# Score maxima of two heads in one reduction over both PSUM banks; first loads, a small product and the written orders changed with it

## The chip, the cores and the metric

One core of a Trainium2 chip runs the kernel. The metric is the device time of one execution in microseconds (us); lower is better. A profile of one execution stands beside the times.

## What is computed

The input is 64 sequences of 64 channels and 256 positions. They go through four sub-layers in a row: an 8-head cross-attention with rotary positions, a feed-forward layer with ternary weights and 8-bit activations, a one-head cross-attention with a mask, and a gated feed-forward layer with ternary weights by groups of 64.

```python
# sub-layer A, heads of 8 channels: the part that the change touches
scores = einsum('bhtc,bhsc->bhts', q, k) / sqrt(8)
p      = softmax(scores, axis=-1)          # the kernel takes a row maximum out before exp
out    = einsum('bhts,bhsc->bhtc', p, v)
# sub-layer B: the scales of the 8-bit activations that the small product feeds
gamma_x = clip(max(abs(x), -1), 1e-5);  gate = silu(bit_linear(x, gate_w));  val = bit_linear(x, val_w)
y = bit_linear(gate * val, out_w)          # its scale contains gamma_x squared
```

## The kernel before, in words

Two sequences make a pair, whose 128 channels fill the partitions; there are 32 pairs. Every engine works through a list of named steps such as `mx3:7` (step kind `mx`, part 3, pair 7). The lists are written out by hand for each engine: HEAD for the first pairs, ORDER for a steady period that LOOP repeats with a growing pair number, and TAIL for the last pairs. The order on an engine is fixed by its list; semaphores between the kinds of steps hold a step until what it needs is there. The SP list issues nearly all DMAs.

For a pair the chain is: load and normalise (`xP`, `bsP`, `mvP`, `rsP`, `xnP`), projections (`proj`, `v`), rotary (`r1`, `r2`, `rot`, `hi`, `lo`, and `kq`, six DMAs into KQ), scores for the maxima (`S`, 16 heads of the pair, line 617), their row maxima (`mx`, line 1120), the maxima turned and put back into KQ as one more row (`mxp`, `mxc` line 804, `md`), scores again the other way round with the maximum subtracted (`T`, line 625), exp (`E`, line 799), probabilities times values (`pv`, line 639), the division (`u`, `sg`, `rc`, `or`, `om`), output projection (`y`, `x1`). Sub-layer B follows three periods behind (`bsB`, `sxB`, `xr`, `xq`, `bg`, `bv`, `Bg`, `Bv` line 691, `Bd`), then the second attention (`xcT`, `sc`, `wx`, `pD`, `pT`, `ro`), then sub-layer C (`Cg`, `Cu` line 728, `Cd` line 739) up to seven periods behind, and `st` stores the pair.

PSUM has eight banks of 512 fp32 columns. Two hold the first scores (`psS`), two the second (`psT`), four all else (`psW`; BANKS says which step uses which of the four). `S` of head n writes 128 x 512 scores of one head (two matmuls of 256 columns) into bank n % 2 of psS, and `mx` of head n reduces that bank to two maxima per partition:

```python
after(pe, "mx", p, n - 2)                                  # line 614: S of head n waits for mx of head n - 2
after(dve, "S", p, n)                                      # line 1117: mx of head n waits for S of head n
m = nc.vector.tensor_reduce(mx[:, p % 2, :, 4 * (n % 4) + n // 4],
                            psS[:, n % 2, :].rearrange("p (c s) -> p c s", c=NK), AX.X, ALU.max)
```

So one bank is filled while the other is reduced. `sxB` (lines 1186 to 1197) makes the scales of sub-layer B in instructions on one column; the second product of them is a SCALAR_TENSOR_TENSOR with two tensors in SBUF (line 1195).

At the start SP loads the table with the identity (`tab`), the biases, the small weights (`wsm`), the first x and the first context; ACT issues at once the six weight loads of 1 MB each (lines 746 to 755). TensorE, VectorE and GpSimd each wait for all set-up work before their first listed step. Ternary weights are made from the raw ones between the steps of the first pairs (`c`, `ab`, `ra`, `gm`, `gv`, `qa`, `rn`, `cl`, `qb`, `fx`, `tn`, `tc`, `fr`, `ct`).

## Time and profile before

| | |
|---|---|
| median of 3 runs | 837.59 us (830.35 to 840.47) |
| the profiled execution | 840.63 us, its span 838.8 us |
| busy share of the span, PE / DVE / ACT / POOL | 91% / 90% / 84% / 76% |
| `psS` maxima, line 1120 | 512 instructions, 333.3 us busy |
| SCALAR_TENSOR_TENSOR of line 1195 | 32 instructions, 20.8 us busy |

The span runs from the first to the last instruction. A busy share counts an instruction from its start to its end, also where the next one has begun, so that a busy engine can still hold work that would fit closer. TensorE's matmuls overlap, and two score matmuls in different row groups run side by side.

### The profile page before, as it was taken

The page shows a single profiled execution, that of the slowest core. Times are in us where ns is not written, and L with a number is a line of the kernel's source. Part 1 is how long each engine was busy: PE and PEld are TensorE (multiplying, and loading weights), DVE is VectorE, ACT ScalarE, POOL GpSimd, SP SyncE. Part 2 cuts the span into 40 slices and gives each one's busy share as a digit, 9 for nine tenths or more (in the row PEclk, how much of TensorE's full clock was granted, in tenths as well). Part 3 has the DMA queues.
Part 4 walks back from the last instruction along what each step waited for, and adds up shares of the span by engine and source line. Part 5 has one row for each costly group of instructions (what it writes and reads, how often), then busy time and mean ns, then how long its engine had stood idle before and what let it go on. Part 6 is the DMA issues. An engine that isn't in the chain of part 4 may idle for free. (4 is left out here: it accounts for less than half of the span.)

```text
span 838.8 us, 22126 instructions
## 1 busy us (share of the span) xinstructions
PE 763.0 (91%) x6898; PEld 398.9 (48%) x6898; DVE 752.7 (90%) x1636; ACT 701.4 (84%) x1447; POOL 634.2 (76%) x1139
## 2 busy tenths in 40 slices
PE   2677899999999999999999999999999989898886
PEld 1333444454555554555555555555545445444444
DVE  5688899999899999999999999999989989787865
ACT  3888888888799998999989999999979889688644
POOL 3827566788888887888888888888878877677632
PEclk9557899999999999999999999999999999899989
DMA  9401222244443444454544444544443434344230
GB/s 311 133 21 39 59 75 77 65 114 88 94 115 95 115 97 106 109 112 108 113 109 106 112 110 114 115 99 112 109 97 101 104 84 112 72 91 97 57 69 20
DMA packets 197952, 82.59 MB, mean 98 GB/s; under 512 B 139710, under 2 KB 196670, under 8 KB 197836
## 3 DMA queue, kind: packets, MB, share of 16 engines
q1 hardware_dynamic: 193260, 74.63, 38.1%
q10 hardware_dynamic: 4576, 6.55, 2.4%
q8 instruction: 56, 0.92, 0.5%
q14 instruction: 60, 0.49, 0.2%
HBM read 28.15 MB, written 4.69 MB: 39 GB/s over the span
## 5 line engine op out<-in xcount | busy, mean ns | idle before, releaser
L1120 DVE TENSOR_REDUCE mx<-psS 128x2 f32<-128x512 f32 x512 | 333.3, 679 | 21.0 <-PE psS L617 19.9
L799 ACT ACTIVATE prob<-psT 128x512 f32<-128x512 f32 x512 | 292.4, 603 | 23.2 <-PE psT L625 15.4
L617 PE MATMUL psS<-KQ 31*128 31x256 f16 x1024 | 137.7, 284 | 15.1 <-DVE mx L1120 12.1
L639 PE MATMUL psW<-prob,vst 128*32 128x256 f32 x2048 | 143.0, 400 | 0.0
L728 PE MATMUL psW<-guT,xT 128*128 128x512 bf16 x512 | 133.5, 390 | 6.3 <-DMA xT<-stage 5.1
L625 PE MATMUL psT<-KQ 32*128 32x256 f16 x1024 | 129.4, 280 | 3.9 <-ACT prob L799 3.0
L639 PEld LDWEIGHTS psW<-prob,vst 128*32 128x32 f32 x2048 | 55.2, 112 | 61.5 <-issue 34.6
L728 PEld LDWEIGHTS psW<-guT,xT 128*128 128x128 f16 x512 | 43.3, 99 | 72.8 <-issue 38.8
L1004 POOL TENSOR_TENSOR hqB<-wide,rnd 128x512 bf16<-128x512 f32 x60 | 63.4, 1058 | 14.7 <-ACT wide L847 14.4
L617 PEld LDWEIGHTS psS<-KQ 31*128 31x128 f16 x1024 | 40.0, 93 | 72.4 <-DVE mx L1120 46.1
L1018 POOL TENSOR_TENSOR stage<-stage 128x512 f16<-128x512 f32 x60 | 69.6, 1161 | 2.6 <-ACT stage L908 0.5
L691 PE MATMUL psW<-tern,xqT 128*128 128x512 bf16 x256 | 70.5, 389 | 0.0
L739 PE MATMUL psW<-pT,stage 128*128 128x256 bf16 x512 | 66.0, 273 | 2.0 <-DMA stage<-stage 1.4
L625 PEld LDWEIGHTS psT<-KQ 32*128 32x128 f16 x1024 | 42.1, 93 | 44.6 <-ACT prob L799 27.0
L739 PEld LDWEIGHTS psW<-pT,stage 128*128 128x128 f16 x512 | 47.8, 98 | 18.2 <-issue 6.6
L1243 DVE SCALAR_TENSOR_TENSOR stage<-stage,psW 128x512 f32<-128x512 f32 x64 | 43.1, 681 | 14.2 <-ACT stage L900 13.4
L813 ACT COPY uA<-psW 128x512 f32<-128x512 f32 x64 | 37.7, 588 | 19.9 <-PE psW L639 19.8
L652 PE MATMUL psW<-cP,wsm 128*128 128x256 f32 x128 | 46.9, 451 | 7.4 <-DMA cP<-in_ctx 6.4
L842 ACT ACTIVATE stage<-psW,sB 128x512 f32<-128x512 f32 x64 | 44.0, 688 | 11.3 <-PE psW L691 9.8
L900 ACT ACTIVATE stage<-psW 128x512 f32<-128x512 f32 x64 | 38.0, 595 | 17.8 <-PE psW L728 17.6
L998 POOL TENSOR_TENSOR r<-pc,tab 128x512 f32<-128x512 f32 x32 | 40.7, 1273 | 15.3 <-ACT pc L818 15.3
L847 ACT ACTIVATE wide<-wide,sB 128x512 f32<-128x512 f32 x64 | 46.6, 733 | 0.4 <-DVE sB L1220 0.2
(190 smaller groups left out, 1791.0 us busy)
## 6 DMA issues: line engine op xcount, KB each, us to landing
KQ<-hl SPq DMA_DIRECT2D x192, 64.0 KB, 1.9
xP<-in_x SPq DMA_DIRECT2D x32, 128.0 KB, 2.2
cP<-in_ctx SPq DMA_DIRECT2D x32, 128.0 KB, 2.1
xA<-in_x SPq DMA_DIRECT2D x32, 128.0 KB, 2.6
cB<-in_ctx SPq DMA_DIRECT2D x32, 128.0 KB, 2.3
oV<-uA SPq DMA_DIRECT2D x32, 128.0 KB, 2.1
out<-x SPq DMA_DIRECT2D x32, 128.0 KB, 2.1
oR<-rden_d SPq DMA_DIRECT2D x120, 32.0 KB
```

Of the source, the lines that this page charges most:

```text
L617: m = nc.tensor.matmul(psS[:, n % 2, T * k:T * k + T], KQ[p % DEEP][r, 1, g, 128 * k:128 * k + 128], KQ[p % DEEP][r, 0, g, :], start=True, ...
L625: m = nc.tensor.matmul(psT[:, n % 2, T * k:T * k + T], KQ[p % DEEP][r, 0, g, 128 * k:128 * k + 128], KQ[p % DEEP][r, 1, g, :], start=True, ...
L639: m = nc.tensor.matmul(bank[32 * j:32 * j + 32, :], vst[p % DEEP][:, k, 4 * n + j, :], prob[:, (4 * n + j) % 8, k, :], start=(k == 0), sto ...
L652: m = nc.tensor.matmul(bank[:, T * f:T * f + T], wqk[:, j, :], (cP, xnP)[f][:], start=True, stop=True)
L691: m = nc.tensor.matmul(psW[:, BANK[f"{kind.lower()}{n}"], :], xqT[:, k, :], (gT if kind == "Bg" else vT)[:, k, 512 * n:512 * n + 512], sta ...
L728: m = nc.tensor.matmul(bank, xT[:, NK * part + k, :], w[:, k, :], start=(k == 0 and part == 0), stop=(k == NK - 1 and part == 1))
L739: m = nc.tensor.matmul(psW[:, BANK["Cd0"], 0:T], hT[:, 8 * part + c, :], pT[:, c, :], start=(c == 0 and part == 0), stop=(c == 7 and part ...
L799: m = nc.scalar.activation(flat(prob[:, n % 8, :, :]), psT[:, n % 2, :], ACT.Exp, scale=float(HC) ** -0.5)
L847: m = nc.scalar.activation(hrB[:, 512 * n:512 * n + 512], hB[:, 512 * n:512 * n + 512], ACT.Copy, scale=sB[:, p % 2, 8:9], bias=ROUND)
L1004: m = nc.gpsimd.tensor_tensor(hqB[:, h], hrB[:, h], rnd[:].broadcast_to([P, 512]), ALU.subtract)
L1018: m = nc.gpsimd.tensor_tensor(hhl[:, 1, n, :], hC[:, n, :], hhl[:, 0, n, :], ALU.subtract)
L1120: m = nc.vector.tensor_reduce(mx[:, p % 2, :, 4 * (n % 4) + n // 4], psS[:, n % 2, :].rearrange("p (c s) -> p c s", c=NK), AX.X, ALU.max)
```

## The change

Two heads are reduced by one instruction of 128 x 1024 over both banks of psS, which writes four maxima per partition; there are 8 of them in a pair and not 16. `S` of heads 2n and 2n+1 wait for the maxima of the two heads before them, and a reduction waits for both of its heads. psS still has two banks. The product of line 1195 becomes a TENSOR_SCALAR, whose two factors are both pointer scalars (one tensor, two columns). At the start, x comes first and the table last on SP; ACT waits for the biases and small weights, then issues two weight loads, and the other four become steps `wl` in its list; TensorE does its first projections and `v` before it waits for the table; the identity copies of GpSimd (`id`) and two of the three memsets of vst (`vm`) become steps. All five lists and the table of banks are written anew. The new kind `hot` stands in no list.

```diff
-PARTS = {**{k: NH for k in ("S", "mx", "T", "E")}, "pv": NG,
+PARTS = {**{k: NH for k in ("S", "T", "E")}, "mx": NH // 2, "pv": NG,
...
-SET_POOL, SET_DVE = 13, 2 * DEEP + 2
+SET_POOL, SET_DVE = 13, DEEP + 3
 ORDER = {
-    "pe": """ro:-5 pv0:-1 T6:-1 S8:0 T7:-1 bg0:-3 S9:0 proj0:2 Bg0:-3 S10:0 T8:-1 T9:-1 S11:0 pv1:-1 Bd:-4 bv0:-3
-           S12:0 bv1:-3 S13:0 T10:-1 bg1:-3 T11:-1 Bv0:-3 Bg1:-3 Bv1:-3 S14:0 T12:-1 S15:0 T13:-1 y:-2 proj1:2 mxp:0
-           T14:-1 S0:1 S1:1 T15:-1 pv2:-1 Cg0:-5 pv3:-1 tn0:0 tn4:-4 Cg1:-5 xcT:-4 gm:1 S2:1 T0:0 S3:1 T1:0 Cu0:-5
-           v:2 sc:-4 S4:1 T2:0 S5:1 T3:0 tn2:-2 Cu1:-5 tn1:-1 tn3:-3 tn5:-4 Cd0:-6 pT:-4 S6:1 T4:0 S7:1 T5:0 Cd1:-6""",
-    "dve": """mx6:0 x4:-7 bsP:3 x3:-5 mx7:0 bsC:-5 fx2:-4 mx8:0 mx9:0 ct0:-2 ct1:-2 mvC:-5 cl1:0 r1:2 mx10:0 mx11:0
-           aB0:-3 mvP:3 x2:-4 mx12:0 mx13:0 bsD:-4 hB0:-3 mvD:-4 cl0:1 ra2:1 mx14:0 ct2:-2 mx15:0 aB1:-3 bsB:-2
-           cl2:-1 hB1:-3 fx1:-1 mvB:-2 fx0:0 mx0:1 val:2 amH:-3 mx1:1 ra1:2 sx:-3 gv:1 aC0:-5 amB:-2 aC1:-5 mx2:1
-           mx3:1 sxB:-2 wx:-4 mx4:1 mx5:1 bs:0 rc:-1 hC0:-5 hC1:-5 ra0:3""",
...
+    "pe": """pv2:-2 Cg0:-6 pv3:-2 Cg1:-6 S2:0 S3:0 T0:-1 gm:0 T1:-1 xcT:-5 v:1 Cu0:-6 sc:-5 S4:0 S5:0 T2:-1 tn3:-4
+           T3:-1 tn0:-1 Cu1:-6 tn4:-5 tn5:-5 Cd0:-7 tn2:-3 T4:-1 S6:0 S7:0 T5:-1 pT:-5 Cd1:-7 ro:-5 pv0:-1 T6:-1
+           T7:-1 S8:0 S9:0 bv0:-3 bg0:-3 proj0:2 Bg0:-3 T8:-1 T9:-1 tn1:-2 S10:0 S11:0 pv1:-1 Bd:-4 T10:-1 S12:0
+           S13:0 bv1:-3 T11:-1 bg1:-3 Bv0:-3 Bg1:-3 Bv1:-3 T12:-1 S14:0 S15:0 T13:-1 y:-2 proj1:2 mxp:0 T14:-1 S0:1
+           T15:-1 S1:1""",
+    "dve": """mvB:-3 ct0:-1 amH:-4 cl1:-1 mx0:0 fx0:-1 ct2:-3 sx:-4 aC0:-6 amB:-3 mx1:0 sxB:-3 hC0:-6 wx:-5 mx2:0
+           aC1:-6 ra2:1 fx2:-4 rc:-2 ra0:2 gv:0 cl0:1 hC1:-6 mx3:0 x4:-7 bsP:3 cl2:-2 x3:-5 bsC:-5 mx4:0 mvC:-5 r1:2
+           mx5:0 aB0:-3 mvP:3 ct1:-2 ra1:2 x2:-4 mx6:0 bsD:-4 hB0:-3 mvD:-4 bs:-2 mx7:0 fx1:-1 aB1:-3 bsB:-2 hB1:-3
+           val:2""",
...
-    "dve": """bsP:0 mvP:0 r1:0 ra0:0 bsP:1 mvP:1 bsP:2 mvP:2 ra1:0 r1:1 mx0:0 mx1:0 mx2:0 gv:0 mx3:0 mx4:0 mx5:0 mx6:0
-           mx7:0 cl0:0 mx8:0 bs:0 mx9:0 mx10:0 mx11:0 mx12:0 bsP:3 mx13:0 r1:2 mx14:0 mvP:3 mx15:0 fx0:0 mx0:1 mx1:1
...
+    "dve": """bsP:0 mvP:0 vm0:0 r1:0 ra0:0 bsP:1 mvP:1 ra1:0 bsP:2 r1:1 mvP:2 ra2:0 mx0:0 mx1:0 mx2:0 mx3:0 gv:0 mx4:0
+           bsP:3 mvP:3 r1:2 mx5:0 cl0:0 mx6:0 mx7:0 vm1:0 mx0:1 fx0:0 bsP:4 mx1:1 mx2:1 r1:3 mx3:1 mx4:1 mvP:4 cl1:0
+           mx5:1 bs:0 mx6:1 mx7:1 val:0 mx0:2 mx1:2 ct0:0 mx2:2 cl2:0 mx3:2 rc:0 mx4:2 ct1:0 fx1:0 r1:4 mx5:2 mx6:2
+           ct2:0 bsP:5 mvP:5 bsB:0 mvB:0 mx7:2 amB:0 mx0:3 sxB:0 mx1:3 mx2:3 rc:1 mx3:3 mx4:3 bsP:6 mx5:3 mx6:3 r1:5
...
+    "act": """xnP:0 wl0:0 vst:0 wl1:0 c0:0 pc:0 wl2:0 c1:0 hi:0 xnP:1 wl3:0 c2:0 ab0:0 pc:1 ab1:0 vst:1 ab2:0 xnP:2
+           rn0:0 hi:1 rn1:0 xnP:3 fr0:0 pc:2 mxc:0 md:0 rn2:0 E0:0 E1:0 E2:0 E3:0 vst:2 E4:0 E5:0 E6:0 fr1:0 E7:0
...
-BANKS = ("v tn0 tn1 bv1 tn5 Cg1 Cd0 lh0 lh1 lx",
-         "proj0 gm mxp y Bd tn4 Cg0 Cu1 lz0",
-         "pv2 bg0 bg1 tn3 ro Cu0",
-         "proj1 pv0 tn2 bv0 xcT sc pT lq lz1")
+BANKS = ("v pv0 bv1 tn4 Cg0 Cu1 lq lh1 lz0",
+         "proj0 mxp y tn2 Bd ro Cg1 lx",
+         "gm tn0 pv2 tn1 bg0 bg1 tn3 tn5 Cu0 Cd0",
+         "proj1 bv0 xcT sc pT lh0 lz1")
...
-            sp.dma_start(tab[:], c_tab).then_inc(S["tab_in"], 16)
+            sp.dma_start(xP[:], x_p[0]).then_inc(S["xP"], 16)
             sp.dma_start(small[:], biases).then_inc(S["c_in"], 16)
             sp.dma_start(wsm[:], w_small).then_inc(S["c_in"], 16)
-            sp.dma_start(xP[:], x_p[0]).then_inc(S["xP"], 16)
             sp.dma_start(cP[:], ctx_p[0]).then_inc(S["cP"], 16)
+            sp.dma_start(tab[:], c_tab).then_inc(S["tab_in"], 16)
...
-            pe.wait_ge(S["tab_in"], 16)
-            pe.wait_ge(S["set_pool"], SET_POOL)
             pe.wait_ge(S["set_dve"], SET_DVE)
-
+            settled = False
+
+            hot_banks = iter(HOT_BEFORE)
             for name, kind, n, p in PROGRAM["pe"]:
+                if not settled and kind not in ("proj", "v"):
+                    pe.wait_ge(S["tab_in"], 16)
+                    pe.wait_ge(S["set_pool"], SET_POOL)
+                    settled = True
...
-                    after(pe, "mx", p, n - 2)
+                    after(pe, "mx", p, n // 2 - 1)
...
-                    after(pe, "mx", p, NH - 1)
+                    after(pe, "mx", p, NH // 2 - 1)
...
+            act.wait_ge(S["c_in"], 16 * 2)
             for i, (raw, part) in enumerate(((stage[:, 3, :], gu_w[0:HID, :]), (late[0], gu_w[HID:2 * HID, :]))):
                 nc.scalar.dma_start(raw.rearrange("p (r d) -> p r d", r=8), part.rearrange("(r p) d -> p r d", p=P))\
                     .then_inc(S[f"w1_{i}"], 16)
-            nc.scalar.dma_start(late[1].rearrange("p (r h) -> p r h", r=2), p_w.rearrange("(r p) h -> p r h", p=P))\
-                .then_inc(S["w1_2"], 16)
-            for i, w in enumerate((gate_wT, val_wT)):
-                nc.scalar.dma_start(stage[:, i, :].rearrange("p (k h) -> p k h", k=2),
-                                    w.rearrange("(k p) h -> p k h", p=P)).then_inc(S[f"w0_{i}"], 16)
-            nc.scalar.dma_start(stage[:, 2, :].rearrange("p (k d) -> p k d", k=8),
-                                out_wT.rearrange("(k p) d -> p k d", p=P)).then_inc(S["w0_2"], 16)
-            act.wait_ge(S["c_in"], 16 * 2)
...
+                if kind == "wl":
+                    raw, w = ((late[1].rearrange("p (r h) -> p r h", r=2), p_w.rearrange("(r p) h -> p r h", p=P)),
+                              (stage[:, 0, :].rearrange("p (k h) -> p k h", k=2), gate_wT.rearrange("(k p) h -> p k h", p=P)),
+                              (stage[:, 1, :].rearrange("p (k h) -> p k h", k=2), val_wT.rearrange("(k p) h -> p k h", p=P)),
+                              (stage[:, 2, :].rearrange("p (k d) -> p k d", k=8),
+                               out_wT.rearrange("(k p) d -> p k d", p=P)))[n]
+                    nc.scalar.dma_start(raw, w).then_inc(S[("w1_2", "w0_0", "w0_1", "w0_2")[n]], 16)
...
+                    if 0 < p < DEEP:
+                        act.wait_ge(S["set_dve"], SET_DVE + p)
...
-            for i in range(DEEP):
-                nc.vector.memset(vst[i][:], 1.0).then_inc(S["set_dve"], 1)
+            nc.vector.memset(vst[0][:], 1.0).then_inc(S["set_dve"], 1)
             nc.vector.memset(ones[:], 1.0 / (T * HID)).then_inc(S["set_dve"], 1)
             nc.vector.memset(brow[:], 0.0).then_inc(S["set_dve"], 1)
             dve.wait_ge(S["c_in"], 16 * 2)
-            dve.wait_ge(S["tab_in"], 16)
             dve.wait_ge(S["bv_ready"], 1)
             nc.vector.tensor_tensor(bo_c[:], psW[:, 0, 0:1], small[:, 4:5], ALU.add).then_inc(S["set_dve"], 1)
             dve.wait_ge(S["set_dve"], SET_DVE)
-            dve.wait_ge(S["set_pool"], SET_POOL)
 
...
+                if kind == "vm":
+                    nc.vector.memset(vst[n + 1][:], 1.0).then_inc(S["set_dve"], 1)
+                    continue
...
-                    after(dve, "S", p, n)
+                    after(dve, "S", p, 2 * n + 1)
                     if n == 0:
                         after(dve, "mxp", p - 2)
-                    m = nc.vector.tensor_reduce(mx[:, p % 2, :, 4 * (n % 4) + n // 4],
-                                                psS[:, n % 2, :].rearrange("p (c s) -> p c s", c=NK),
-                                                AX.X, ALU.max)
+                    first = 8 * (n % 2) + n // 2
+                    m = nc.vector.tensor_reduce(mx[:, p % 2, :, first:first + 5:4].rearrange("p c h -> p h c"),
+                                                psS[:].rearrange("p h (c s) -> p h c s", c=NK), AX.X, ALU.max)
...
-                    nc.vector.scalar_tensor_tensor(out=sc[:, 5:6], in0=sc[:, 1:2], scalar=sc[:, 1:2],
-                                                   in1=gam_q[:, 1:2], op0=ALU.mult, op1=ALU.mult)
+                    nc.vector.tensor_scalar(sc[:, 5:6], sc[:, 1:2], sc[:, 1:2], gam_q[:, 1:2], ALU.mult, ALU.mult)
```

## Rows read from the trace of the kernel before

**Rows 1.** The page's first part: busy time, share of the span, instructions.
```profile
PE 763.0 (91%) x6898; PEld 398.9 (48%) x6898; DVE 752.7 (90%) x1636; ACT 701.4 (84%) x1447; POOL 634.2 (76%) x1139
```

**Rows 2.** Stages by `mxs`: count, duration min/median/max, first and last start.
```profile
L804 ACT ACTIVATE mxs<-psW x10: 356/372/373, 49.7 to 246.2; 16x256 f16<-16x256 f32 x10
...
L804 ACT ACTIVATE mxs<-psW x17: 372/372/373, 246.2 to 602.3; 16x256 f16<-16x256 f32 x17
...
L804 ACT ACTIVATE mxs<-psW x7: 356/372/373, 602.3 to 745.2; 16x256 f16<-16x256 f32 x7
```

**Rows 3.** Stretches: length, busy of PE, PEld, DVE, ACT, POOL; clock, DMA, GB/s.
```profile
50.00:246.00 196.00, 181.80 (x1638) 88.71 (x1636) 177.41 (x367) 167.43 (x331) 137.87 (x225) 0.91 0.31 74
246.00:602.00 356.00, 347.02 (x3394) 187.51 (x3392) 348.59 (x785) 325.35 (x705) 308.53 (x561) 1.00 0.47 108
602.00:745.00 143.00, 135.26 (x1259) 68.68 (x1257) 128.95 (x286) 119.67 (x261) 110.19 (x203) 0.96 0.42 97
745.00:839.00 94.00, 75.98 (x546) 42.61 (x544) 64.73 (x137) 57.75 (x127) 50.02 (x107) 0.95 0.29 65
```

**Rows 4.** The same view, four steady periods: the first, and the sum.
```profile
492.10:514.10 22.00, 21.68 (x216) 11.76 (x220) 21.63 (x50) 20.33 (x45) 19.28 (x35) 1.00 0.46 112
...
sum 87.90, PE 86.86 PEld 47.00 DVE 86.59 ACT 81.42 POOL 77.11; mean PE 21.71 PEld 11.75 DVE 21.65 ACT 20.36 POOL 19.28
```

**Rows 5.** Waits from 470 to 580 us: in total, times, longest.
```profile
POOL rsC L958 <- DVE mvC L1171: 3.2, 5, 0.9
...
PE psW L716 <- ACT pD L887: 1.0, 3, 0.4
...
PEld psS L617 <- DVE mx L1120: 5.4, 14, 0.4
```

**Rows 6.** Groups by form: busy, mean ns, idle before and its releaser.
```profile
L1120 DVE TENSOR_REDUCE mx<-psS 128x2 f32<-128x512 f32 x512 | 333.3, 679 | 21.0 <-PE psS L617 19.9
...
L1185 DVE TENSOR_REDUCE sB<-wide 128x1 f32<-128x1024 f32 x32 | 38.7, 1208 | 0.1
...
L1195 DVE SCALAR_TENSOR_TENSOR sB<-sB,gam_q 128x1 f32<-128x1 f32 x32 | 20.8, 649 | 0.0
```

**Rows 7.** Timeline: start, length, engine, line, operation.
```profile
404.34 1.21 DVE L1185 TENSOR_REDUCE sB<-wide 128x1 f32<-128x1024 f32 x1
...
405.47 0.68 DVE L1120 TENSOR_REDUCE mx<-psS 128x2 f32<-128x512 f32 x1
...
408.47 1.28 DVE L1120 TENSOR_REDUCE mx<-psS 128x2 f32<-128x512 f32 x2
...
409.49 1.27 POOL L1010 TENSOR_TENSOR rot<-r 128x512 f32<-128x512 f32 x1
...
409.67 0.14 DVE L1193 TENSOR_SCALAR sB<-sB 128x1 f32<-128x1 f32 x1
...
409.98 0.80 DVE L1195 SCALAR_TENSOR_TENSOR sB<-sB,gam_q 128x1 f32<-128x1 f32 x1
...
410.70 0.15 DVE L1197 RECIPROCAL sB<-sB 128x1 f32<-128x1 f32 x1
```

**Rows 8.** Lines 1195 and 1194, each: duration ns min/median/max, first and last start.
```profile
L1195 DVE SCALAR_TENSOR_TENSOR sB<-sB,gam_q x32: 208/765/1057, 97.9 to 782.1; 128x1 f32<-128x1 f32 x32
...
L1194 DVE TENSOR_SCALAR sB<-sB,gam_q x32: 212/214/216, 97.7 to 782.0; 128x1 f32<-128x1 f32 x32
```

**Rows 9.** Timeline of the start, with the idle time before in brackets.
```profile
9.35 0.59 PE L587 MATMUL psW<-small,wsm 128*128 128x1 f32 x2 [9.35 <-DMA wsm<-in_w_small]
...
10.08 0.16 DVE L1057 TENSOR_TENSOR bo_c<-psW,small 128x1 f32<-128x1 f32 x1 [3.46 <-PE psW L587]
...
23.15 1.19 PE L652 MATMUL psW<-cP,wsm 128*128 128x256 f32 x2 [6.41 <-DMA cP<-in_ctx]
...
28.32 0.39 PE L617 MATMUL psS<-KQ 31*128 31x256 f16 x4 [1.41 <-DMA KQ<-hl]
...
32.71 0.59 PE L602 MATMUL psW<-wsum,ones 128*128 128x4 f32 x2
```

## What the change was predicted to do

> **What bounds the kernel now.** I read the page's busy shares first. TensorE (PE) and VectorE (DVE) are both at 90% or a little more, ScalarE (ACT) is at 84% [rows 1], so the shares alone do not name a bound. Next I cut the span by stage, with the maxima product `mxs` as the clock of the pairs [rows 2]. The first comes at 49.7 us. Nine more pairs take 196.5 us (21.8 each), the repeated order's sixteen pairs take 356.1 us (22.3 each), the last six take 142.9 us (23.8 each), and 93.6 us of the span follow the last maxima. In the repeated part PE and DVE are both busy 98%, in the two parts around it DVE is at 90 to 91% and PE at 93 to 95% [rows 3]. In four undisturbed periods of 22.0 us, DVE has 0.3 us idle and PE 0.26 us [rows 4].
>
> So I looked at how much of these busy times must be there. DVE's do not add up without gaps: two maxima back to back start at 408.47 and the next instruction starts at 409.67, so one occupies DVE for 0.60 us, though it is listed with 0.68 [rows 7]. In PE the waits of weight loads tell more than its busy time: in five periods they wait 5.4 us for maxima, and PE itself 1.0 us for `pD` [rows 5]. DVE paces the loop, with PE close behind it. GpSimd (POOL) waits little for anyone, and it works through chains of small dependent steps. Its 19.3 us of 22.0 leave at most 2.7 us, and ACT's 20.4 us leave 1.6 [rows 4].
>
> **The maxima.** 512 instructions of 512 columns become 256 of 1024. The trace has a reduction of 1024 columns, in SBUF: listed 1208 ns [rows 6], and the next instruction starts 1.13 us after it [rows 7]. Two maxima occupy 1.20 us, so each pair of heads saves 0.07 us, which makes 0.56 us in a pair and 18 us in all. By listed durations it would be 2 x 679 - 1208 = 150 ns, 38 us in all. The lower end is nothing, if crossing the bank or writing four scattered maxima costs as much as one start. I take 18, because occupancy is what an engine at 98% gives back.
>
> Here a rule of the Trainium skill can be weighed ("VectorE: DVE Perf Modes", the section on the TRN2 errata): it gives a VectorE instruction from PSUM 120 cycles plus its columns, at 0.96 GHz. Its 120 cycles would save 0.125 us in a pair of heads, an estimate of 32 us in all. The rows show that half of this already overlaps with the neighbour.
>
> **The small product.** Line 1195 takes 649 ns in the mean, 765 in the median and 208 at least [rows 6, 8]. In the timeline it starts at 409.98 while POOL's 128x512 sum runs from 409.49 to 410.76, and it ends at 410.78 [rows 7]: it waits for POOL. The TENSOR_SCALAR before it, on the same columns, takes 212 to 216 ns in all 32 pairs, whatever POOL does [rows 8]. The new form is the same kind with a second pointer scalar. I price it at 0.21 us: 20.8 - 32 x 0.21 = 14 us. The ends are 0, if it waits for POOL too, and 18 us by the median. The page "SBUF — State Buffer" of the Trainium skill (section on the two separate sides) says that VectorE and GpSimd share one pair of ports by an exclusive lock, taken by a VectorE instruction with two SBUF tensors or in a 2-port perf mode. For line 1195 the trace agrees; should the new TENSOR_SCALAR run in such a mode, the rule would take the 14 us away, and line 1194 is the row against that.
>
> DVE thus loses 0.56 + 0.44 = 1.0 us in a pair, and needs about 21 us where it had 22.
>
> **The bank that no longer alternates.** A pair of heads now needs: both maxima done, four matmuls of `S`, the reduction. Four such matmuls take 0.39 us [rows 9], and a handover from PE to DVE 0.14 us (9.94 to 10.08) [rows 9], so a refill that nothing covers costs DVE 0.39 + 2 x 0.14 = 0.67 us. Before, the other bank's reduction covered it. The new DVE list puts other work between the maxima: `hC0 wx`, `aC1 rc hC1`, `x4 bsP x3 bsC`, `mvC r1`, `aB0 mvP x2` and so on. The shortest of these gaps, `mvC r1`, holds 2 x 0.4 us and a small one, so each is longer than a refill. On PE the new list has about 2 us of other work between two blocks of `S`, which is longer than the 1.2 us of a reduction with its two handovers. In the loop I charge nothing. If that cover went in one of eight, it would be 0.67 us in a pair, 21 us in all. In pair 0 there is no cover: `mx0` to `mx3` stand together in the list. I charge 8 x 0.4 = 3 us there, between 0 and 8 x 0.67 = 5.
>
> **What PE can take.** The gain of the loop ends where PE ends. The certain part is its idle 0.26 us [rows 4]. The upper end adds the weight loads' wait for maxima, 5.4 / 5 = 1.1 us [rows 5], most of which lies under running matmuls. The new PE list also moves `pT` a block of scores further from `sc`, so that its wait for `pD` (1.0 / 5 = 0.2 us) should go, and keeps more scores in blocks. I take 0.6 us in a period, between 0.26 and 1.0 (all that DVE gives). Sixteen pairs: 10 us. Nine pairs before them, where DVE also makes the ternary weights: 0.55 each, 5 us. The last six, with DVE at 90%: 0.5 each, 3 us. After the last maxima no term of the change is left but the new lists; DVE has 29 of 94 us idle there [rows 3]. I charge 0, within 4 us either way.
>
> **The start.** The first matmul waits until 9.35 us for the small weights, which share the queues with 6 MB of raw weights, and the second context holds PE for 6.4 us until 23.15 [rows 9]. With the raw weights behind the small ones the first should come some 4 us earlier. The product over all weight sums (32.71 us, line 602) waits for the last raw weight [rows 9], and the same bytes must arrive, now issued later; pair 0 has it in the middle of its scores. So a part of the 4 us comes through, and I take 6 us for the queue and the second context together, less the 3 us above: 3 us net, between -3 and +7. The four weight loads are now steps in ACT's list and cost it their issue; the moved memsets and copies are the same instructions later, under the loads. SP's and POOL's lists have the same steps in another order and can hold one another; that, and the new table of banks, is in the range.
>
> **Sum.** 10 + 5 + 3 + 3 = 21 us less than the profiled execution's 840.6, 819.6. The median of the runs lies 3.0 below that execution: 817.
>
> **Rivals.**
> - All that DVE gives arrives (PE's list packs better): 1.0 us x 31 pairs = 31, and 6 at the start: 37 less, 801 on the median. For it: the weight loads' waits. Against it: ACT with 20.4 of 22.0, which would be at 97%. Chance 0.17.
> - PE is the bound already: only 0.26 us x 31 = 8, and 2 at the start: 827. For it: PE's 98.8% in four periods. The same time results if the joined reduction saves nothing or the new product waits for POOL, so the case that the change doesn't do what it says is in here. Chance 0.28.
> - The single set of banks decides: PE and DVE take turns. Its place is the refill inside a pair; its price 0.67 us for each uncovered one against 1.0 us saved per pair, so it decides from two in eight on. With half of them uncovered, 4 x 0.67 - 1.0 = 1.7 us in a pair in the loop and less than half of that elsewhere, some 35 us in all with nothing at the start: 872; with three, 20: 857. DVE's 19.9 us of waiting for scores, with two banks, speak for it [rows 6]. The Trainium skill ("Trainium Kernel Development and Optimization", Best Practices) advises double buffering, which is this rival's side. Chance 0.10, and I give it 860.
> - My forecast: 0.45, its own range 808 to 828.
>
> **Numbers.** A difference under 2% (16.8 us, 820.8 to 854.3) can't be told from no change in this kernel. Faster by more: 0.65 of my case, all of the first rival, little of the second: 0.49. Slower: two thirds of the third: 0.08. Within: 0.43. The range leaves out half of the best case below and the turn-taking above: 800 to 841.
>
> **What would show it.** Line 1120 with 256 instructions of about 1.21 us, the next instruction starting 1.13 us on; its replacement of line 1195 at 0.21 us in every pair; `mxs` 21.6 us apart in the loop; PE's idle under 0.2 us in a period, DVE's idle near 1 us, put down to scores (line 617) or projections. A first matmul near 5 us. Wrong would be a period of 22 us or more with DVE waiting for scores before most reductions, a reduction above 1.36 us, the product still at 0.6 us, or a clock below 1.00 in the loop.

## The result and the profile after

| | before | after |
|---|---|---|
| median | 837.36 us (830.35 to 840.47, 4 runs) | 845.18 us (841.00 to 847.11, 4 runs) |
| ratio, 95% interval | | 1.0128 [1.0079, 1.0176] |
| the profiled execution's span | 838.8 us | 842.1 us |

The changed kernel is slower by one per cent, a difference that these runs separate from zero though it is under 2%: its fastest execution is slower than the slowest of the kernel before. The forecast was 817 us and the range ended at 841. Medians are of all runs, while the ratio is an estimate from the fast ones and not the quotient of the two medians (1.0093 here). The two profiled executions lie 3.3 us apart by their spans where the medians lie 7.8 apart, so the stages below account for part of the loss.

The page's busy times of the kernel after (engine, us, share, instructions), beside [rows 1]:

```profile
PE 749.6 (89%) x6898; PEld 394.2 (47%) x6898; DVE 728.5 (87%) x1380; ACT 698.7 (83%) x1447; POOL 633.5 (75%) x1139
```

Its groups by form (busy, mean ns, idle before and the releaser), beside [rows 6]:

```profile
L1140 DVE TENSOR_REDUCE mx<-psS 128x4 f32<-128x1024 f32 x256 | 311.5, 1217 | 38.4 <-PE psS L628 37.7
...
L1216 DVE TENSOR_SCALAR sB<-sB,gam_q 128x1 f32<-128x1 f32 x32 | 8.5, 265 | 0.0
```

The work did fall as intended: VectorE is busy 24.2 us less. The time did not follow. What VectorE lost in work it spends waiting, 17.8 us of it for scores (37.7 us after 19.9). The stages by `mxs`, beside [rows 2] (count, duration, first and last start):

```profile
L816 ACT ACTIVATE mxs<-psW x10: 357/373/374, 47.6 to 248.7; 16x256 f16<-16x256 f32 x10
...
L816 ACT ACTIVATE mxs<-psW x17: 373/373/374, 248.7 to 611.6; 16x256 f16<-16x256 f32 x17
...
L816 ACT ACTIVATE mxs<-psW x7: 357/373/373, 611.6 to 751.5; 16x256 f16<-16x256 f32 x7
```

The first comes 2.1 us earlier, nine pairs take 201.1 us instead of 196.5, the sixteen of the loop 362.9 instead of 356.1, the last six 139.9 instead of 142.9, and 90.6 us of the span follow instead of 93.6. So the loop lost 6.8 us where it was to give 10. Its stretch in the view of stretches, beside [rows 3]:

```profile
248.00:611.00 363.00, 341.89 (x3394) 185.07 (x3393) 336.12 (x658) 324.44 (x706) 308.26 (x561) 1.00 0.49 106
```

TensorE did the same 3394 matmuls at the full clock (1.00, 2.4 GHz) and has fallen from 97 to 94% busy, VectorE from 98 to 93%. Nobody is at a bound; everybody waits for somebody. These are the waits of the loop (248 to 611 us) with a named releaser, in the kernel after: in total, times, longest.

```profile
POOL xqB L1000 <- DVE sB L1217: 23.5, 16, 3.5
...
PE psW L739 <- DMA xT<-stage: 15.4, 16, 2.5
ACT stage L914 <- PE psW L739: 13.5, 14, 2.7
DVE mx L1140 <- PE psS L628: 11.4, 16, 2.0
DVE stage L1263 <- ACT stage L914: 11.0, 11, 2.6
```

The same view of the kernel before, over its loop (248 to 602 us):

```profile
DVE stage L1243 <- ACT stage L900: 3.4, 6, 1.0
...
PE psW L728 <- DMA xT<-stage: 1.2, 2, 0.7
```

Read them as a chain. The gate matmuls of layer C wait once in every pair for the transpose `xT` (15.4 us, before 1.2). ScalarE waits for those matmuls and VectorE for ScalarE, VectorE's list is late, and GpSimd waits for its `sxB` once in every pair. SP in turn waits once in every pair for what GpSimd and ScalarE make of it, `xqB` (248 to 610 us):

```profile
SPq L337 <- POOL xqB L1004: 16.6, 16, 1.1
...
SPq L561 <- ACT xqB L850: 13.4, 16, 0.9
```

The scores' share, 11.4 us in 16 pairs of 8 reductions, is small: a turn-taking over the banks would show here, and in TensorE's waits for `mx`, of which this stretch has none; neither shows. The transpose is issued by SP. Its timeline in one period of the kernel after (start, length, queue, line, operation):

```profile
415.47 1.25 SPq L561 DMA_TRANSPOSE xqT<-xqB  x1
416.82 0.53 SPq L543 DMA_DIRECT2D rden_d<-rden  x1
417.44 0.59 SPq L531 DMA_DIRECT2D oV<-uA  x1
418.12 1.27 SPq L565 DMA_TRANSPOSE hqT<-hqB  x1
419.48 2.85 SPq L548 DMA_DIRECT2D oR<-rden_d  x4
422.44 3.82 SPq L527 DMA_DIRECT2D KQ<-hl  x6
426.30 0.59 SPq L579 DMA_DIRECT2D out<-x  x1
427.06 2.25 SPq L571 DMA_TRANSPOSE xT<-stage  x1
```

And TensorE at its end:

```profile
431.06 1.02 PE L739 MATMUL psW<-guT,xT 128*128 128x512 bf16 x4 [0.27 <-DMA xT<-stage]
```

From the transpose of `xqB` on, SP issues 16 transfers one behind the other with at most 0.17 us between two, and `xT` is the last of them, 11.6 us after the first. The one ahead of it is the store of pair p-8, for which nobody stands waiting here: 0.59 us and a small gap, 0.76 us in all. In the old list the store stood near the beginning:

```diff
-    "sp": """xP:4 cP:3 st:-8 sm:9 ov:-1 d1:-1 qT:-2 ht:-3 or:-1 kq:2 xT:-4 cB:-3 xA:0 hT:-5 br:-1 sg:0""",
+    "sp": """xP:3 qT:-3 d1:-2 ov:-2 ht:-4 or:-2 kq:1 st:-8 xT:-5 xA:-1 br:-2 sm:26 cB:-4 hT:-6 sg:-1 cP:3""",
```

Together with the waits above this reads as a circuit: `xT`, gate matmuls, ScalarE, VectorE, `sxB`, GpSimd, `xqB`, SP's issues, `xT`. In a circuit every 0.76 us is paid in every pair. That is theory L, after the lists: the place of the transpose in SP's list costs the time. Theory B, after the banks, was the prediction's third rival: the single set of banks costs.

### The profile page after: what moved, and what is told of

The parts are those of the page before. It is cut to its first block and busy times, and to the rows that moved or that the text cites. A ratio compares the mean times of both kernels' runs of the same rounds, so it can differ in the third digit from the quotient of the medians.

```text
span 842.1 us, 21875 instructions
## 1 busy us (share of the span) xinstructions
PE 749.6 (89%) x6898; PEld 394.2 (47%) x6898; DVE 728.5 (87%) x1380; ACT 698.7 (83%) x1447; POOL 633.5 (75%) x1139
## 5 line engine op out<-in xcount | busy, mean ns | idle before, releaser
L1140 DVE TENSOR_REDUCE mx<-psS 128x4 f32<-128x1024 f32 x256 | 311.5, 1217 | 38.4 <-PE psS L628 37.7
L739 PE MATMUL psW<-guT,xT 128*128 128x512 bf16 x512 | 135.6, 395 | 23.4 <-DMA xT<-stage 22.9
L628 PE MATMUL psS<-KQ 31*128 31x256 f16 x1024 | 111.9, 282 | 22.3 <-DVE mx L1140 12.3
L636 PEld LDWEIGHTS psT<-KQ 32*128 32x128 f16 x1024 | 39.6, 93 | 70.4 <-ACT prob L811 43.4
L1023 POOL TENSOR_TENSOR hqB<-wide,rnd 128x512 bf16<-128x512 f32 x60 | 63.4, 1060 | 11.6 <-ACT wide L861 11.6
L628 PEld LDWEIGHTS psS<-KQ 31*128 31x128 f16 x1024 | 33.8, 93 | 61.3 <-DVE mx L1140 29.6
L750 PEld LDWEIGHTS psW<-pT,stage 128*128 128x128 f16 x512 | 50.0, 100 | 13.1 <-DVE stage L1271 2.0
L1033 POOL TENSOR_TENSOR hl<-rot,hl 128x512 f16<-128x512 f32 x32 | 37.1, 1159 | 24.7 <-ACT hl L842 21.8
L1271 DVE SCALAR_TENSOR_TENSOR stage<-stage,hsc,psW 128x512 f32<-128x512 f32 x64 | 45.9, 718 | 5.4 <-PE psW L739 3.7
```

Source lines behind the costliest of these rows:

```text
L628: m = nc.tensor.matmul(psS[:, n % 2, T * k:T * k + T], KQ[p % DEEP][r, 1, g, 128 * k:128 * k + 128], KQ[p % DEEP][r, 0, g, :], start=True, ...
L636: m = nc.tensor.matmul(psT[:, n % 2, T * k:T * k + T], KQ[p % DEEP][r, 0, g, 128 * k:128 * k + 128], KQ[p % DEEP][r, 1, g, :], start=True, ...
L739: m = nc.tensor.matmul(bank, xT[:, NK * part + k, :], w[:, k, :], start=(k == 0 and part == 0), stop=(k == NK - 1 and part == 1))
L750: m = nc.tensor.matmul(psW[:, BANK["Cd0"], 0:T], hT[:, 8 * part + c, :], pT[:, c, :], start=(c == 0 and part == 0), stop=(c == 7 and part ...
L1023: m = nc.gpsimd.tensor_tensor(hqB[:, h], hrB[:, h], rnd[:].broadcast_to([P, 512]), ALU.subtract)
L1140: m = nc.vector.tensor_reduce(mx[:, p % 2, :, first:first + 5:4].rearrange("p c h -> p h c"), psS[:].rearrange("p h (c s) -> p h c s", c=N ...
```

## The experiments

All of them, each with its median, its ratio to the kernel before run beside it on the same chip (whose median was 833.86 to 835.42 us beside e1 to e15), the loop's sixteen pairs by `mxs`, and TensorE's wait for `xT` in the whole execution (us, times). The last two columns are of the one profiled execution, which lies up to 5.8 us from the kernel's median (e11 5.8 and e5 5.5 us above, e3 3.3 and e1 3.2 us below):

| kernel | median | ratio, 95% interval | loop | `xT` |
|---|---|---|---|---|
| before | 837.36 | | 356.1 | 5.1, 6 |
| after | 845.18 | 1.0128 [1.0079, 1.0176] | 362.9 | 22.9, 23 |
| e1 before, new product | 829.79 | 0.9923 [0.9886, 0.9959] | 347.1 | 3.4, 3 |
| e2 before, joined | 905.96 | 1.0855 [1.0800, 1.0910] | 363.4 | 2.0, 2 |
| e3 after, split | 839.74 | 1.0061 [1.0024, 1.0098] | 359.6 | 19.0, 20 |
| e4 after, `xT` before `st` | 824.35 | 0.9871 [0.9830, 0.9911] | 349.1 | 9.8, 11 |
| e5 e4, split | 825.37 | 0.9858 [0.9810, 0.9906] | 353.8 | 8.1, 7 |
| e6 e4, old product | 824.84 | 0.9870 [0.9814, 0.9926] | 345.4 | 9.1, 9 |
| e7 `xT` before `kq` | 913.14 | 1.0910 [1.0857, 1.0963] | 429.8 | 5.9, 5 |
| e8 before, `st` late | 1037.68 | 1.2408 [1.2344, 1.2473] | 559.3 | 5.6, 3 |
| e9 `st` last | 825.59 | 0.9905 [0.9874, 0.9937] | 347.4 | 7.0, 7 |
| e10 `xA` before `xT` | 846.15 | 1.0134 [1.0096, 1.0172] | 365.8 | 26.5, 22 |
| e11 before, `cB` before `xT` | 847.92 | 1.0174 [1.0134, 1.0214] | 370.7 | 16.9, 15 |
| e12 e4, head changed | 826.49 | 0.9906 [0.9872, 0.9940] | 350.1 | 7.6, 8 |
| e13 e4, split, old product | 824.66 | 0.9888 [0.9854, 0.9922] | 348.7 | 7.1, 8 |
| e14 after, `d1 ov` first | 858.87 | 1.0309 [1.0267, 1.0350] | 379.2 | 19.7, 19 |
| e15 e4, `d1 ov` first | 846.35 | 1.0159 [1.0124, 1.0194] | 372.7 | 5.3, 5 |

**What stands ahead of the transpose.** e4 exchanges two entries of SP's repeated list:

```diff
-or:-2 kq:1 st:-8 xT:-5 xA:-1
+or:-2 kq:1 xT:-5 st:-8 xA:-1
```

> The changed kernel with two entries of SP's steady list exchanged, so that the transpose of xT (pair p-5) is issued before the store of pair p-8 instead of behind it. Theory L: xT is issued about 0.6 us earlier in each of 16 loop pairs, gate/up matmuls wait less for it (22.9 us falls towards 13), and the time falls by 3 to 8 us, to 837 to 842. Theory B: the wait for xT was in the shadow of the scores, and the time stays within 2 us of 845.

It gave far more than expected: 0.9871 against the changed kernel's 1.0128, some 21 us. In its loop the transpose now follows `kq` at once, and the waits of the circuit went together:

```profile
POOL xqB L1000 <- DVE sB L1217: 7.7, 11, 1.8
...
DVE mx L1140 <- PE psS L628: 5.0, 12, 0.7
PE psW L739 <- DMA xT<-stage: 4.8, 5, 2.0
...
ACT stage L914 <- PE psW L739: 3.3, 4, 1.5
...
DVE stage L1263 <- ACT stage L914: 1.9, 3, 1.1
```

The wait for scores fell with them, though the banks are the same single set, so it was mostly a consequence. The loop gained 13.8 us, 0.86 in each pair, near the 0.76 that was moved. The remaining 6 us lie outside the loop, where the lists are the same: 1.1 less in the nine pairs, 2.3 in the last six, 1.2 behind them and 1.6 at the start. The stages there vary by 2 or 3 us among kernels with the same lists, so I assign them to nothing. TensorE's granted clock does not explain the 21 us: three of e4's six executions have a mean of 0.952 to 0.956, as the four of the kernel after (0.949 to 0.955), and take 822 to 826 us against 841 to 847. e10 puts another transfer there and takes the store away, e9 takes the store to the end of the list:

```diff
-or:-2 kq:1 st:-8 xT:-5 xA:-1 br:-2
+or:-2 kq:1 xA:-1 xT:-5 st:-8 br:-2
```

> The changed kernel with the store out of the way but another load, xA of 0.57 us on SP, in its place ahead of the transpose of xT. Theory L (any issue of 0.6 us there costs the same, whatever it moves): about 845 us again, 838 to 848, with about 20 waits for xT of about 20 us in sum. Rival (it was the store itself, through the buffer x4 or the DMA traffic that it makes at that time): 822 to 829 us, as in e4.

```diff
-kq:1 st:-8 xT:-5 xA:-1 br:-2 sm:26 cB:-4 hT:-6 sg:-1 cP:3
+kq:1 xT:-5 xA:-1 br:-2 sm:26 cB:-4 hT:-6 sg:-1 cP:3 st:-8
```

> The changed kernel with the store of pair p-8 at the very end of SP's steady list, behind cP, where SP waits for others anyway, so that neither xT nor hT stands behind it. Theory L (only the place of the transpose in SP's chain mattered, and PE bounds the loop once it is early): the same as with the store right behind xT, 820 to 827 us. Rival (SP's chain still bounds the loop at 21.5 us a period): the 0.6 us per period that the store takes goes as well, 810 to 819 us.

Side by side on one chip they came out at 846.15 and 825.59 us, with 18.4 us between their loops, 1.15 a pair. It is not the store, its bytes or its buffer: another issue of 0.6 us in that place costs the same 20 us. And behind the transpose the store's place makes no difference that can be measured (e4 and e9). e11 tries the same in the old lists, with the old reductions:

```diff
-or:-1 kq:2 xT:-4 cB:-3 xA:0 hT:-5
+or:-1 kq:2 cB:-3 xT:-4 xA:0 hT:-5
```

> The kernel before with the load cB (0.58 us on SP) and the transpose of xT exchanged in SP's steady list. In the trace of before the gate matmuls start 3.0 us after the transpose's issue, which lands about 0.5 us ahead of them, so a shift of 0.6 us just uses up the slack. Theory L: 835 to 845 us with 10 to 20 waits for xT of 5 to 15 us, a smaller loss than in the new lists because the old ones leave 0.5 us. Rival (the old lists bear it, VectorE bounds their loop): within 0.4% of before.

It lost 14.6 us in its loop, 0.9 a pair, and took over the sign of the kernel after (in the whole execution; 11 of the waits are in the loop):

```profile
PE psW L728 <- DMA xT<-stage: 16.9, 15, 2.2
```

So the loss needs neither the join nor the new lists; the slack of 0.5 us that I had granted the old ones did not soften it.

The circuit can be measured in SP's timelines of the loop (means of its 16 pairs, worked out from the starts and the landings). From the issue of the transpose of `xqB` to the landing of `xT` it takes 15.4 us in the kernel after and 15.5 in e10, 14.1 in e4 and in e9; from that landing round to the next transpose of `xqB` it takes 7.5, 7.4, 7.6 and 7.5 us. In the old lists the two parts are 13.0 and 9.3 us before, 14.0 and 9.4 in e11. The rest of the round stays as it is, and the whole part in which the transfer was put ahead is added to the period. This also answers why the price is above 0.76 us: of the 1.24 us between the kernel after and e4, 0.65 is the later issue, and 0.59 is that the transpose lands later after its issue. In the view of `xT` over the loop, the kernel after and then e4:

```profile
DMA to landing us min/median/max: 2.5/2.8/4.7
```

```profile
DMA to landing us min/median/max: 2.5/2.5/4.0
```

Right behind the store, `xA` or `cB` (the kernel after, e3, e10, e11, e14) the mean is 2.9 to 3.3 us, and 4 to 8 of 16 transposes take over 3 us; right behind the copies to KQ (the kernel before, e1, e2, e4 to e6, e9, e12, e13, e15) it is 2.5 to 2.7 us, with 1 to 3 of 16. Where SP pauses ahead of it, 11 us in e8 and 3 us in e7, the mean is 2.5. What holds the transpose up behind another transfer was not tested.

**What the join and the product are worth.** e1 and e2 put each alone into the kernel before, e3 takes the join out of the one after:

```diff
-nc.vector.scalar_tensor_tensor(out=sc[:, 5:6], in0=sc[:, 1:2], scalar=sc[:, 1:2],
-                               in1=gam_q[:, 1:2], op0=ALU.mult, op1=ALU.mult)
+nc.vector.tensor_scalar(sc[:, 5:6], sc[:, 1:2], sc[:, 1:2], gam_q[:, 1:2], ALU.mult, ALU.mult)
```

> The kernel before with one edit: the product of line 1195 as a tensor_scalar with two pointer scalars. Both theories expect the same of it, since it is common ground: the instruction should last about 0.27 us as in the changed kernel instead of 0.65, VectorE should lose about 0.38 us of work or waiting per pair, 12 us over the execution, and the time should move by -5 to 0 us (ratio 0.994 to 1.000). If it is slower than before by more than 3 us, the order of VectorE against GpSimd for their shared port is a cause of its own.

In the old lists the product gives 0.8%, 5.3 us between the medians of those runs (the loops of the two profiled executions are 9 us apart), and its row is as in the kernel after:

```profile
L1195 DVE TENSOR_SCALAR sB<-sB,gam_q 128x1 f32<-128x1 f32 x32 | 8.5, 264 | 0.0
```

e2 (the same edit of `mx`, `S` and `mxp` as in the change; in each list the joined maximum stands where the second head's stood):

```diff
-mx6:0 x4:-7 bsP:3 x3:-5 mx7:0 bsC:-5 fx2:-4 mx8:0 mx9:0
+x4:-7 bsP:3 x3:-5 mx3:0 bsC:-5 fx2:-4 mx4:0
```

> The kernel before, its own five lists, start and old product, with the joined reduction alone: one 1024-column maximum stands where the second head's stood, and a score matmul waits for the reduction of the two heads before it. Theory L (the new lists cost the time: the xT transpose is issued late on SP's queue, the gate/up matmuls wait for it, and that wait is carried to ScalarE and VectorE; the join itself is neutral): 832 to 840 us, ratio to before 0.995 to 1.003, about 6 waits for xT as before. Theory B (one set of banks costs: in each of 256 turns the refill of 0.67 us is uncovered, VectorE waits for scores): 848 to 870 us, ratio 1.013 to 1.04, VectorE's wait for psS well over 40 us, waits for xT unchanged.

Worse than Theory B had it, and mostly in the nine pairs: 242.6 us instead of 196.5, with these waits there (53 to 296 us):

```profile
PEld psS L617 <- DVE mx L1121: 51.7, 47, 2.6
ACT prob L799 <- PE psT L625: 35.5, 37, 3.0
DVE mx L1121 <- PE psS L617: 35.0, 32, 3.9
PE psS L617 <- DVE mx L1121: 34.3, 29, 2.4
```

This is turn-taking as the rival described it: each waits for the other by turns, about 35 us both ways. In the loop the same kernel loses 7.3 us only. The old lists have the scores of a pair of heads apart in both stretches. What differs is VectorE's list: in the first pairs it has up to four joined maxima in a row (`mx1:1` to `mx4:1`), in the loop always other work between two, which was the prediction's condition for a covered refill. So the single set of banks is harmless only with lists that cover the refill; which property of the lists does it was not tested by itself. The Trainium skill ("Trainium Kernel Development and Optimization", Best Practices) advises double-buffering, there for overlapping DMA with compute. For two PSUM banks this run bears the advice out, and e5, with the new lists, shows nothing of it.

e3 (the edit in reverse, two reductions of 512 columns back to back over alternate banks, the new lists):

```diff
-mx0:0 fx0:-1 ct2:-3 sx:-4 aC0:-6 amB:-3 mx1:0
+mx0:0 mx1:0 fx0:-1 ct2:-3 sx:-4 aC0:-6 amB:-3 mx2:0 mx3:0
```

> The changed kernel with its new lists, new start and new product, but two reductions of 512 columns again, back to back at the place of the joined one, each over its own banks, so that there is a second buffer again. Theory L: the transpose xT is as late as in the changed kernel (about 20 waits, some 20 us in the gate/up matmuls), so it stays at 843 to 850 us (ratio to before 1.007 to 1.016). Theory B: with the second buffer back the refill is covered, VectorE's wait for psS falls from 38 us to about 20, and the time falls to 828 to 838 us.

It lies between the two theories, in neither's range: 20 waits for `xT` as L had it, but 5 us faster than the kernel after, the two intervals overlapping a little. With the late transpose the second buffer may be worth half a per cent; this is not settled. The clean comparison is with the early transpose: e5 is e3's edit on e4, e6 the old product on e4, e13 both.

> The changed kernel with the transpose of xT ahead of the store (as in e4) and two reductions of 512 columns over alternate banks in place of the joined one. It prices the join where the late transpose no longer hides it. Theory L (SP's chain of issues sets the loop's period): the join was worth next to nothing and its missing second buffer cost something, since the split lists took 843 to 838 us with the late transpose; 820 to 826 us, within 0.4% of e4, VectorE busy about 15 us more, its wait for psS about 20 us. Theory J (the join pays once the transpose is early): 829 to 836 us, with VectorE busy 744 us and no waits to spare.

> The changed kernel with the transpose of xT ahead of the store, and the old scalar_tensor_tensor product. In the kernel before the new product alone gave 0.8%. Theory L: the same price here or less, 824 to 831 us, with the product again about 0.65 us where GpSimd holds the port. Rival: the gain of e4 is mostly the product's, then it comes out at 833 us or more.

> The lists and the start of the changed kernel with xT ahead of the store, and neither the joined reduction nor the new product. If the reordered lists and the start alone make the gain, it stays within 0.5% of the kernels with both (824 to 828 us), though VectorE has some 25 us more to do. If VectorE's work counts once both are missing, 831 to 838 us, no better than before.

The three give 825.4, 824.8 and 824.7 us where e4 has 824.4. The join is worth nothing that can be measured, in either direction, and so is the product; the intervals of e4 and e13 are each 3 us wide to either side, so a few us of gain or loss stay possible. The lists, the table of banks and the start, which were not taken apart, make the gain, with VectorE busy 740.0 us in e13 and 728.5 in e4. The product's row in e13 says why it stopped paying:

```profile
L1216 DVE SCALAR_TENSOR_TENSOR sB<-sB,gam_q 128x1 f32<-128x1 f32 x32 | 8.0, 249 | 0.0
```

The old instruction takes 249 ns here instead of 649 [rows 6], less than the new one's 265. In the trace of before, GpSimd has an instruction of over 0.9 us under way at the start of 25 of the 32 products, in e13 at 4 of 32, and the other 28 of e13 last 0.21 us each. The new lists have GpSimd waiting for this very chain at that time. The new instruction takes 0.26 to 0.27 us also where GpSimd has such an instruction under way, 6 of 32 in the kernel after and 23 of 32 in e1. The Trainium skill ("SBUF — State Buffer", the section on the two separate sides) puts the old wait down to a lock on a shared port, which the trace bears out by this too.

**Other places in SP's queue.** Four other orders lost, and each shows another thing that an in-order queue ties together. e7:

```diff
-kq:1 st:-8 xT:-5
+xT:-5 kq:1 st:-8
```

> The changed kernel with SP's steady list changed further: the transpose of xT (p-5) ahead of the six copies to KQ and the store. Theory L: the copies take 3.8 us on SP, but xl is ready only 1.3 us before the transpose in e4, so at most 1.3 us per period can be had, and KQ moves later by 1.3 us or more, which the last score matmuls of the pair take if they have room; 812 to 824 us. Rival: SP waits for xl with the six copies behind it, the scores of the next pair wait for KQ, and it comes out at 826 to 836 us.

The rival's sign, at a price that neither had. In the loop SP waits 36.5 us, once a pair, for `xl` with the six copies behind it:

```profile
SPq L337 <- POOL stage L1041: 36.5, 16, 2.6
```

and the period is 27.3 us in most pairs. `xl` is ready only after `kq` is due, and TensorE now stands waiting for KQ (its score weight loads 45.2 us in 13 times between 250 and 600 us). e8 was to carry the late store into the old lists:

```diff
-xP:4 cP:3 st:-8 sm:9 ov:-1 d1:-1 qT:-2 ht:-3 or:-1 kq:2 xT:-4
+xP:4 cP:3 sm:9 ov:-1 d1:-1 qT:-2 ht:-3 or:-1 kq:2 st:-8 xT:-4
```

> The kernel before with only the store of pair p-8 moved in SP's steady list to where the new lists have it, right ahead of the transpose of xT. Theory L (the issue of 0.6 us ahead of the transpose lengthens each period by about as much): xT is issued 0.6 to 0.7 us later in 16 pairs, about 15 more waits for it, and the time rises by 6 to 14 us to 841 to 850. Rival: the late transpose only hurts in the new lists, whose tensor list comes to it sooner, and the time stays at 833 to 838.

Both missed by 190 to 200 us, since I had overlooked a wait in the code: `x4` of a pair goes into the buffer that the store two pairs earlier reads. In the old lists VectorE comes to `x4` before SP comes to the moved store. VectorE stands there 10.8 us in each period (172.1 us in 16 times), with everything behind it:

```profile
411.75 0.48 DVE L1257 SCALAR_TENSOR_TENSOR x<-psW,msC,x 128x256 f32<-128x256 f32 x1 [11.08 <-issue]
```

SP had issued the store at 409.72. The releaser is named "issue" because the profile has no event for that semaphore. e8 therefore says nothing on `xT`; e11 took its place. e14 leaves the store ahead of `xT` and shortens the wait at the head of the run, e15 does it on e4:

```diff
-xP:3 qT:-3 d1:-2 ov:-2 ht:-4
+xP:3 d1:-2 ov:-2 qT:-3 ht:-4
```

> The changed kernel with the store still ahead of the transpose of xT, but d1 and ov (0.34 to 0.53 and 0.59 us of issue) moved ahead of the transpose of xqB. In the changed kernel's loop SP waits about 1 us a period for xqB (13.4 us in 16 times for its cast, 16.6 us for its quantization) with d1 and ov behind it. Chain theory (the unbroken run of issues from that transpose to the one of xT sets the period): two issues of about 1 us in sum go into time in which SP waits anyway, xT is issued up to 1 us earlier, and the time falls about as in e4, to 822 to 830 us. Place theory (only what stands right before xT matters, or d1 and ov are not ready and the transpose of xqB is now late behind them): 842 us or more.

> Both edits of SP's list at once: xT ahead of the store, and d1 and ov ahead of the transpose of xqB. If SP's chain still takes part in the period of 21.5 to 21.9 us, the time falls below e4, to 812 to 820 us. If TensorE bounds the loop by then (21.4 us busy per period in e4), it stays at 820 to 827 us.

Both lost: e14 in the place theory's range, e15 beyond both of its forecasts. e14 does not speak for the place alone, since the place theory's other condition came true in it as well: its TensorE waits 17.6 us in 16 times for `xqT`, and SP waits 44.4 us in 15 times for `rden`. In e15's loop `rden` is ready late, SP waits for it, and `xqT` is late behind `d1`. First SP, then TensorE:

```profile
SPq L543 <- DVE rden L1175: 46.1, 16, 3.0
```

```profile
PE psW L697 <- DMA xqT<-xqB: 19.4, 16, 2.4
```

The wait for `xT` is small in e15 (5.3 us), so this is a second transfer that sets the period when it is late, not evidence against the first.

**The head.** e12 moves two entries on e4:

```diff
-vst:2 E4:0 E5:0 E6:0 fr1:0 E7:0 hi:2 E8:0
+vst:2 hi:2 E4:0 E5:0 E6:0 fr1:0 E7:0 E8:0
...
-rsP:4 r2:3 rot:3 qb1:0 lo:3 qb2:0
+rsP:4 qb1:0 r2:3 rot:3 lo:3 qb2:0
```

> The lists of e4 (xT ahead of the store) with two entries of the head moved: ScalarE's cast hi of pair 2 ahead of the first probabilities, and GpSimd's qb1 (4.5 us) ahead of the rotation that waits for pc of pair 3. In e4 GpSimd sits idle for 12.5 us for that cast while its 10.5 us of weight work is still to come, and PE and VectorE wait for it later. Theory H (this placement is what costs the new lists 4 us in the first nine pairs): 817 to 822 us, the last score row copy of pair 9 by 243 instead of 246 us. Rival (the nine pairs are bound by VectorE and PE taking turns over one set of banks): 822 to 827 us.

The edit did what it says (GpSimd's longest wait for that cast fell from 12.5 to 6.2 us), and nothing came of it: 826.49 us, e9 beside it 825.59. Theory H has fallen.

## Why the prediction was wrong

**The start and the lists.** The sentence that failed is in the step on the start: SP's and POOL's lists "have the same steps in another order and can hold one another; that, and the new table of banks, is in the range". It was charged 0, for which no row was given. One exchange in SP's list is worth 21 us (e4), and the same amount comes back with another transfer in the place (e10). Without it the changed kernel takes 824 us, inside the forecast's own range of 808 to 828; with it, 845. The profile had the means to see it: the trace of before has the gate matmuls 3.0 us after the issue of `xT` (382.17 after 379.14), with the landing taking 2.5 of them, and the diff shows `st:-8` moved from the third place to the one right ahead of it. The first matmul at 4.96 us was as forecast. The first `mxs` came 2.1 us earlier, and the nine pairs after it took 4.6 us more.

**The maxima.** The duration was right: 1217 ns listed, forecast 1.21. The value was not. It was to be 18 us of VectorE, passed on where TensorE had room. With `xT` early it is worth nothing that can be measured (e4 against e5). The Trainium skill's 120 cycles ("VectorE: DVE Perf Modes") and my 0.07 us per pair of heads differ by 14 us of VectorE's work, and neither amount reached the time.

**The small product.** Forecast 0.21 us, measured 0.265, and no wait for GpSimd, as forecast. 12.3 us of its busy time went instead of 14. In the old lists these were real, and the time fell by 0.8% (e1); in the new ones the wait that it removes is gone already (e13).

**The banks.** Right for the loop, where other work covers the refill, as the prediction had it. VectorE waits 11.4 us for scores in sixteen pairs, and 5.0 once `xT` is early. The place where the rival is true is the nine pairs of the old lists (e2). With nothing left of the join's gain, "no cost" can't be told from "a cost of the same size as its saving".

**What TensorE can take.** The kernels with the new lists and the transpose early (e4 to e6, e9, e12, e13) lie at 824 to 826 us whatever VectorE's work is, with loops of 345 to 354 us; e1's loop of 347.1 us, in the old lists, is of that size too. That is the second rival's forecast (827, TensorE bounds already), not the one that I took. That 824 lies in my own range of 808 to 828 is luck: the saving on VectorE that was to bring it there brought nothing. In four periods of e4 TensorE is busy 21.44 us of 22.0:

```profile
sum 88.00, PE 85.74 PEld 46.59 DVE 84.12 ACT 81.41 POOL 77.08; mean PE 21.44 PEld 11.65 DVE 21.03 ACT 20.35 POOL 19.27
```

That TensorE is the bound there was not shown: no run took work from it, and the circuit's round in e4, 14.1 and 7.6 us, is about as long as its period of 21.8. The other engines' work could be changed without effect (VectorE by 11.5 us), and SP's order could not be bettered by the attempts made.

**What stays open.** Where the nine pairs lose some 4 us against the old lists; it is not the join (e5: 202.3 us, e4: 200.0) and not the wait for the cast (e12). Whether the second buffer is worth half a per cent while the transpose is late (e3). Why `xT` lands later when it is issued right behind another transfer. And what the new table of banks does by itself.

## What to carry to other kernels

When a change rewrites the order of work, read every queue's list against the old one, the queue of an engine that computes nothing among them, and ask for each transfer that somebody waits for what has been put ahead of it; a store that nobody stands waiting for goes behind it. A gain in one engine's work is only worth what the next circuit leaves of it, so measure the new order without the new instruction: here the order and the start alone made all of the gain. And before a step is moved in an in-order queue, list both what it waits for and who waits for its buffer; e7, e8 and e15 lost 22 to 200 us for that.

The version to keep is e4, one exchange away from the changed kernel: 824.35 us, 1.3% under the kernel before; e13, without the join and the new product, is as fast.

## What the runs showed of the hardware

- In the loop of the kernel after, an issue occupies SP's queue for 0.33 to 0.67 us in the median for a plain transfer, for 1.2 to 1.3 us for the transposes of `xqB`, `hqB` and `xT`, and for 2.6 us for the one of line 576. The fifteen issues from the transpose of `xqB` up to that of `xT` take 11.6 us of a period of 22. The Trainium skill ("DMA: Bandwidth & Descriptors", the section on issuing engines) calls the time on the sequencer "usually small relative to the DMA itself"; for one store the trace agrees (0.59 us of issue, 2.0 us to its landing), but fifteen such times in a row are half of the period.
- `xT` lands 2.5 us after its issue in the median in e4, and 2.8 in the kernel after, where the store is issued right ahead of it. With any of three plain transfers right ahead the mean is 2.9 to 3.3 us, without 2.5 to 2.7.
- A TENSOR_SCALAR of one column with two pointer scalars takes 265 ns, with one 214, and the SCALAR_TENSOR_TENSOR that computes the same 210 in the median when GpSimd is idle.
- Two maxima of 512 columns and one of 1024 over two banks differ little: the next instruction starts 1.14 us after the joined one (411.68 to 412.82 in the kernel after), against 1.20 before [rows 7].
